# Two transposes move from behind the gate and up products to the place between them, in the expert stage of a gated attention and mixture-of-experts kernel

## What is computed

```python
def ffn(gw, uw, dw):
    g = jnp.einsum('bsh,ih->bsi', x, gw)
    u = jnp.einsum('bsh,ih->bsi', x, uw)
    return jnp.einsum('bsi,hi->bsh', jax.nn.silu(g) * u, dw)
expert_out = jax.vmap(ffn)(gate_w, up_w, down_w)
output = jnp.einsum('ebsh,bse->bsh', expert_out, combine)
...
x = x + jnp.tanh(g_xattn[0]) * _L0_xattn_ref(ctx_1024, _layernorm(x, axis=-1), mask_BxS2_bk0, ...)
x = x + jnp.tanh(g_ffn[0]) * _L0_ffn_ref(_layernorm(x, axis=-1), ...)
```

## Time and profile before

| | before |
|---|---|
| median of 3 runs | 1449.71 us (1447.56 to 1450.73) |
| the profiled execution | 1448.41 us, its span 1446.8 us |
| TensorE matmuls busy | 1358.9 us, 94% of the span, 13880 matmuls |
| TensorE weight loads busy | 971.7 us (67%) |
| VectorE busy | 1018.4 us (70%) |
| ScalarE busy | 933.8 us (65%) |
| GpSimd busy | 485.5 us (34%) |
| the expert stage | from about 871 us to the end |

### The profile page before, as it was taken

The page is one execution under the profiler, slowest core; times in us unless marked ns, Lnnn a source line. Parts: engine busy times, 40 slices in busy tenths (PEclk is TensorE's granted clock), DMA queues, the critical chain, the costliest instruction groups (busy, mean ns, idle before and its releaser), DMA issues. The chain is left out here.

```text
span 1446.8 us, 41651 instructions
## 1 busy us (share of the span) xinstructions
PE 1358.9 (94%) x13880; PEld 971.7 (67%) x13880; DVE 1018.4 (70%) x2553; ACT 933.8 (65%) x1940; POOL 485.5 (34%) x655
## 2 busy tenths in 40 slices
PE   2999999999999999999999958999999999999996
PEld 1466666666666666666666646887777787777774
DVE  4688888888888888888888875666546663444442
ACT  5677878787887878787887765666656553333331
POOL 4423232433433333434432143333344333222221
PEclk9999999999999999999999968999999999999998
DMA  4010101111111101111100335433376743221461
GB/s 118 27 41 26 42 26 36 41 40 47 39 48 32 54 30 45 42 33 54 38 28 21 114 112 156 115 96 90 87 207 185 234 138 89 32 34 31 118 201 16
DMA packets 54867, 107.16 MB, mean 74 GB/s; under 512 B 10833, under 2 KB 32721, under 8 KB 54673
## 3 DMA queue, kind: packets, MB, share of 16 engines
q0 software_dynamic: 23712, 55.71, 14.9%
q1 hardware_dynamic: 30112, 47.75, 10.5%
q10 hardware_dynamic: 848, 1.07, 0.3%
HBM read 69.16 MB, written 35.34 MB: 72 GB/s over the span
## 5 line engine op out<-in xcount | busy, mean ns | idle before, releaser
L875 ACT ACTIVATE sg<-gP,consts 128x512 f32<-128x512 f32 x126 | 86.5, 686 | 242.9 <-PE uP L1436 242.5
L1353 DVE SCALAR_TENSOR_TENSOR act_h<-uP,consts,sg 128x512 f32<-128x512 f32 x126 | 94.5, 750 | 207.5 <-ACT sg L875 207.1
L1436 PE MATMUL fP<-zTs,ws 128*128 128x112 f16 (+1 forms) x1536 | 221.1, 294 | 7.8 <-DVE zTs L1320 5.2
L987 DVE CUSTOM_DVE_ANT_0 ms<-simP,madd,sim_undo 112x488 f32<-112x488 f32 x256 | 184.0, 719 | 5.0 <-remote 2.5
L1436 PE MATMUL fP<-ws,zTs 128*128 128x512 f16 x768 | 186.8, 379 | 0.5 <-DVE kT L977 0.2
L733 ACT ACTIVATE pr<-ms,nmax 112x488 f32<-112x488 f32 x256 | 179.0, 699 | 4.6 <-DVE nmax L987 1.5
L993 DVE SCALAR_TENSOR_TENSOR pT<-ptP,pT 122x448 f16<-122x448 f32 x256 | 157.5, 615 | 28.8 <-ACT pT L740 28.0
L1436 PE MATMUL yP<-W,aT 128*128 (+1 forms) x1512 | 175.4, 273 | 1.7 <-DVE aT L1359 1.7
L1436 PEld LDWEIGHTS fP<-zTs,ws 128*128 128x128 f16 x1536 | 109.8, 99 | 99.6 <-issue 36.8
L1436 PEld LDWEIGHTS yP<-W,aT 128*128 128x128 f16 x1512 | 147.6, 98 | 33.0 <-issue 3.3
L740 ACT ACTIVATE pT<-ptP 122x448 f16<-122x448 f32 x256 | 137.8, 538 | 41.2 <-PE ptP L1494 37.7
(11 more groups left out here) (220 smaller groups left out, 2502.7 us busy)
## 6 DMA issues: line engine op xcount, KB each, us to landing
raw<-wffn POOLq DMA_DIRECT2D x36, 512.0 KB, 6.1
split_experts<-W POOLq DMA_DIRECT2D x12, 1024.0 KB
W<-split_experts SPq DMA_DIRECT2D x16, 768.0 KB
xc<-ctxt SPq DMA_DIRECT2D x32, 375.0 KB
xt<-routed_rows POOLq DMA_DIRECT2D x63, 129.0 KB, 2.5
raw<-wffn SPq DMA_DIRECT2D x12, 512.0 KB, 5.3
xl<-x SPq DMA_DIRECT2D x32, 112.0 KB
xres<-x SPq DMA_DIRECT2D x32, 112.0 KB
```

Source lines behind the costliest of these rows:

```text
L875: nc.scalar.activation(sg[i][:, :], gP[i][:, :], ACT.Silu, scale=constant(place, 0)).then_inc(s_silu, 1)
L987: nc.vector.tensor_tensor_reduce(out=ms[h % 2][:, :], in0=simP[h % 2][0:S, 0:NK], in1=madd[p][:, :], scale=sim_undo[0:S, 0:1], scalar=3.0e ...
L1353: nc.vector.scalar_tensor_tensor(out=act_h[i][:, :], in0=uP[i][:, :], scalar=constant(place, 2), in1=sg[i][:, :], op0=ALU.mult, op1=ALU.mu ...
L1436: last = nc.tensor.matmul(o, lhs(k, a), rhs(k, c), start=n == 0, stop=n == len(todo) - 1)
```

## The change

In tile t the first-half gate product is followed by the two groups of transposes, and the first-half up product comes behind them. `gate_up` gets an argument that says which of its two products to make; the semaphore `s_gu` is still raised by the last matmul of `uP`. As a side effect the wait for `s_act` is written twice for the first half. ScalarE's, VectorE's, GpSimd's and SyncE's instructions stay as they are.

```diff
-            def gate_up(t, q, i, slot_):
+            def gate_up(t, q, i, slot_, some=(0, 1)):
 
-                if i == 0:
+                if i == 0 and 0 in some:
                     pe.wait_ge(s_xtlo, t + 1)
                 need(pe, s_act, (t - 1) * 2 + (i + 1))
-                for o, w in ((gP[i], WG), (uP[i], WU)):
+                for o, w in [((gP[i], WG), (uP[i], WU))[n] for n in some]:
...
-                last.then_inc(s_gu, 1)
+                if 1 in some:
+                    last.then_inc(s_gu, 1)
...
                 if t < NT:
-                    gate_up(t, q, 0, byte)
+                    gate_up(t, q, 0, byte, (0,))
                 if t > 0:
                     act_T(t - 1, 1)
                 if t < NT - 1:
                     tile_T(t + 1, (t + 1) % XT_BUFS)
+                if t < NT:
+                    gate_up(t, q, 0, byte, (1,))
```

## The result

| | before | after |
|---|---|---|
| median | 1449.3 us (1447.4 to 1451.2, 6 runs) | 1456.0 us (1455.3 to 1459.4, 6 runs) |
| ratio | | 1.0054, 95% interval 1.0044 to 1.0065 |
| span of the profiled execution | 1446.8 us | 1454.1 us |
| period of tiles 5 to 59 | 8.864 us | 8.996 us |
| gate, in the same tiles, mean | 1.35 us | 1.54 us |

What follows compares the result with a forecast made beforehand. A loop through TensorE's sequencer was taken as the bound: 6.34 + 0.08 + 0.25 + 2.34 = 9.01 us a tile, +8.0 us over 57 tiles, profiled 1448.4 to 1456.4; forecast median 1457.5 us, range 1447 to 1474.

Steps and rivals of the forecast that it cites:

- the loop: From `aT` through TensorE's issue of down, gate and up, then silu and `act_h`, to the next `aT`; 8.76 to 8.95 us.
- (a): Issuing the six transposes ahead of up adds sequencer time to each tile's loop: 0.25 us, between 0.17 and 0.47.
- The bound of 0.07 us for a wait: In TensorE's stream, 0.65 us left for three table instructions and six semaphores: at most some 0.07 us each.
- the 6.34 us: Sequencer's time from the end of `aT` to the next tile's transposes, same whether the array waited or not.
- (b): Delay from up's end to `aT` through ScalarE and VectorE: 2.34 us taken, 2.53 for the range.
- (c): New tile period 9.01 us, 9.00 with roundings, against 8.864: +0.14 in 57 tiles, +8.0 us.
- (d): Other effects, such as earlier transposes for ScalarE, next rows' reads, `bP`, late ScalarE tiles and the reload: all 0.
- The faster one: TensorE's sequencer keeps its lead across waits and the transposes refill it: 8.70 us a tile, -9 us, 1441; chance 0.12.
- The much slower one: TensorE's stream cannot run ahead during transposes: 0.67 us in the loop, period 9.43, +32 us, 1482; chance 0.08.
- Cheap transposes: Transposes cost the loop 0.17 us with `aT` always 2.34 after up: period 8.89, +1.5 us, 1451; chance 0.2.
- The wait as the whole cost: Only array and semaphores count: down product waits at most 0.15 us, 0 to 9 us; counted with the main case.

Runs made afterwards that it cites:

- static_after: The changed kernel with TensorE's table of experts written in as constants, so no table read or register addresses; ratio 0.9939 to the kernel before.
- table_in: The kernel before, matmuls in the old order, with the next tile's table read moved from ahead of the down product to between gate and up; ratio 1.0206.
- static_before: The kernel before with TensorE's table of experts written in as constants, so no table read or register addresses; ratio 0.9933.

## Why the prediction was right, point by point

- **What bounds the kernel.** The prediction read the loop through TensorE's sequencer out of the constant time between `aT` and the next transposes. Both ways of cutting it and the constants took the median period to 8.55 us, the sum of the array's pieces in the earlier trace rows, in either order. This step is shown. That it is the sequencer's time for TensorE's own instructions, and not the wait in itself, is shown by `static_after` and by `table_in`.
- **(a) The transposes in the loop.** Taken at 0.25 us between 0.17 and 0.47. The path grew from 6.39 to 6.64: 0.25 by the medians, 0.26 by the means. The sum was right, its make-up was not: two transposes and their waits cost 0.12, four 0.11, and the second wait nothing. The bound of 0.07 us for a wait was also misread: it divided 0.65 us among six waits and three table instructions, but these three stand ahead of the down product's wait, outside the 6.34 us, and `table_in` shows that inside they cost 0.62 alone. That 0.25 was hit so closely is in part luck.
- **(b) The delay of `aT`.** 2.34 us was taken; the median was 2.33, the mean 2.36. Gate slow by 0.25: it was 0.19 on average. Up starved by 0.14: 1.50 - 1.34 = 0.16. The number was right, the reason given for it (2.34 where up is starved to its end, 2.53 where not) is not what the runs show: with constants up is not starved at all, and the delay is 2.33 in the median in both orders. What differs is when `silu` starts, 0.14 us behind up's end in 50 of 55 tiles after and in 16 before; why it is later before is open. The small wait at the down product is there, 0.15 us from the end of `aT` in the median, and the run with constants shows that it costs nothing by itself.
- **(c) The period.** 9.00 us foretold, 8.996 measured; +8.0 us foretold for 57 tiles, +7.3 found in 55.
- **(d) Nothing else.** The tiles in which ScalarE was late stayed late by less: the silu of tile 24 started 1.23 us behind up's end before and 0.66 after. These are the few tenths that the prediction let go in the rounding.
- **The rivals.** The faster one supposed that the sequencer keeps its lead across the wait; gate at 1.54 us against 1.34 says that it does not. The much slower one supposed that it can't run ahead during transposes: the path would have grown by 0.67. "Cheap transposes" was out by 0.1 us a tile. "The wait as the whole cost" would have given about the same time; `static_after` against `static_before` excludes it.

The time was 1456.0 us where 1457.5 was foretold.

What failed was in the experiments: the size of the gain without the loop (new waits for raw weights took a quarter to a third of it), the 3 us for the array's new wait, the price of two transposes against four, and the table read behind the up product.

## What to carry to other kernels

An engine that is shown busy all the time may still be short of instructions: compare the start-to-start time of equal groups where addresses are constants and where registers work them out. Then look for the wait that stops the instruction stream, and count everything that must be issued behind it, since moving instructions to this side of it costs their issue time even if the array has room for them. The cure was to let less stand behind the wait (split it, or have the awaited result made earlier) and to keep slow sequencer work behind long matmuls.

## What the runs showed of the hardware that I had not expected

- A wait on a semaphore that is already met costs TensorE's stream nothing that these runs can tell (a path of 6.66 us with one wait fewer, 6.65 with it).
- Reading one number from a table into TensorE's registers, with its two further instructions and the address arithmetic (`pe.snap` included), held the stream for about 0.62 us between gate and up, as long as eight pairs with register arithmetic (8 x 0.079), and opened a gap of 0.54 us behind up.
- A stream of weight load and matmul pairs on 128 columns keeps 1.34 / 24 = 56 ns a pair through 48 pairs once the addresses are constants, and also with register arithmetic if the sequencer enters them with enough lead; with register arithmetic and no lead it is 79 ns (1.90 / 24).
